# Cross-attention on one core: the output projection in three fp32r passes a block, and the splitting of queries and keys moved from VectorE to ScalarE

## What is computed

```python
q = heads(x @ to_q_w)                                   # (128, 128, 320) @ (320, 320)
for seg, (wk, wv) in zip(segments, weights):            # 77, 4, 4, 43 context rows, width 512
    out += merge(softmax(q @ heads(seg @ wk).T / 4) @ heads(seg @ wv))
result = out @ to_out_w + to_out_b + x                  # (320, 320)
```

## Time and profile before

| | |
|---|---|
| median of 3 runs | 1751.53 us (1750.83 to 1751.56) |
| profiled execution, its own time | 1750.32 us |
| span of its instructions | 1748.5 us |
| busy: PE, DVE, POOL, ACT | 1663.6, 1509.1, 1247.9, 1042.8 us |
| mean granted TensorE clock | 0.990 |

### The profile page before, as it was taken

One profiled execution on the slowest core, in us unless ns is written; L12 is line 12 of the kernel. 1 busy time (PEld: TensorE's weight loads), 2 busy tenths in 40 slices (PEclk: granted clock), 3 DMA queues, 4 the chain that ended last, 5 costly groups with the idle time before them and its releaser, 6 DMA issues.

```text
span 1748.5 us, 48271 instructions
## 1 busy us (share of the span) xinstructions
PE 1663.6 (95%) x15120; PEld 1370.2 (78%) x15120; DVE 1509.1 (86%) x3536; ACT 1042.8 (60%) x1860; POOL 1247.9 (71%) x1452
## 2 busy tenths in 40 slices
PE   6949999999999999999999999999999999999986
PEld 3647888888888888888888888888888888888865
DVE  4238999889999988999998899999889999988997
ACT  1126666666666666666666666666666666666664
POOL 4337777778777777877777887777788777778744
PEclk9979999999999999999999999999999999999999
DMA  8669888888988988898898889889889988987861
GB/s 294 173 168 222 205 221 220 216 219 217 227 201 221 222 215 216 220 224 204 220 224 213 213 222 222 205 222 226 211 213 225 218 208 220 227 209 195 214 128 39
DMA packets 409172, 366.24 MB, mean 209 GB/s; under 512 B 17137, under 2 KB 380210, under 8 KB 404786
## 3 DMA queue, kind: packets, MB, share of 16 engines
q1 hardware_dynamic: 409138, 365.79, 82.4%
HBM read 216.30 MB, written 149.42 MB: 209 GB/s over the span
## 4 chain that ended last, share of the span: by engine, by line
PE 88%; DVE 5%; issue 2%; DMA 1%; ACT 1%; SPq 1%; POOL 1%; ACTq 0%; POOLq 0%
PE job_ps L785 30%; PE ring_ps L851 15%; PE ring_ps L871 12%; PE ring_ps L864 10%; PE job_ps L801 7%; PE s_ps L824 7%; PE job_ps L804 2%; PE ring_ps L752 2%; PE job_ps L812 2%; DVE rest L657 1%; PE job_ps L795 1%; DVE l_seg L667 1%; ACT parts L523 1%; DVE probs L640 1%; DVE m_seg L624 1%
## 5 line engine op out<-in xcount | busy, mean ns | idle before, releaser
L463 POOL TENSOR_TENSOR probs<-probs,rl 128x616 f32<-128x616 f32 (+1 forms) x640 | 628.5, 1004 | 342.1 <-DVE rl L678 340.8
L785 PE MATMUL job_ps<-c_in,w_kv 128*128 128x172 f32 (+1 forms) x2560 | 576.7, 368 | 40.8 <-DVE rest L657 40.8
L550 ACT ACTIVATE pT<-ring_ps 128x512 f32<-128x512 f32 x640 | 378.2, 598 | 356.1 <-PE ring_ps L851 347.3
L785 PEld LDWEIGHTS job_ps<-c_in,w_kv 128*128 128x128 f32 x2560 | 424.4, 190 | 129.8 <-DVE rest L657 48.4
L851 PE MATMUL ring_ps<-ident,probs 128*128 128x128 f32 x2560 | 388.7, 277 | 9.7 <-DVE y L687 8.4
L667 DVE TENSOR_REDUCE l_seg<-probs 128x8 f32<-128x616 f32 (+1 forms) x640 | 385.2, 644 | 7.8 <-ACT probs L541 7.8
L640 DVE TENSOR_TENSOR probs<-s_ps,m_seg 128x616 f32<-128x616 f32 (+1 forms) x640 | 387.5, 647 | 0.0
L624 DVE TENSOR_REDUCE m_seg<-s_ps 128x8 f32<-128x616 f32 (+1 forms) x640 | 371.6, 623 | 3.5 <-issue 0.2
L541 ACT ACTIVATE probs<-probs 128x1024 f32<-128x1024 f32 x320 | 337.7, 1055 | 22.8 <-DVE probs L644 22.8
L851 PEld LDWEIGHTS ring_ps<-ident,probs 128*128 128x128 f32 x2560 | 290.0, 143 | 64.9 <-issue 25.6
L444 POOL TENSOR_TENSOR parts<-rest,zero 128x512 bf16<-128x512 f32 (+1 forms) x192 | 199.0, 1036 | 70.6 <-DVE rest L657 70.6
(11 more groups left out here) (47 smaller groups left out, 1457.0 us busy)
## 6 DMA issues: line engine op xcount, KB each, us to landing
q_all<-q_scratch SPq DMA_DIRECT2D x64, 960.0 KB, 8.4
k_all<-k_scratch SPq DMA_DIRECT2D x64, 960.0 KB, 12.4
c_in<-in_cT SPq DMA_DIRECT2D x32, 1024.0 KB, 5.1
x_raw<-in_xT SPq DMA_DIRECT2D x32, 768.0 KB, 5.1
q_scratch<-parts SPq DMA_DIRECT2D x64, 384.0 KB, 3.0
k_scratch<-parts SPq DMA_DIRECT2D x64, 384.0 KB, 3.0
x_res<-in_x SPq DMA_DIRECT2D x128, 160.0 KB, 3.4
out<-y SPq DMA_DIRECT2D x128, 160.0 KB, 2.8
```

Of the source, the lines that this page charges most:

```text
L463: pool.tensor_tensor(pr[:, :, a:e], pr[:, :, a:e], r[:, :, s:s + 1].broadcast_to((P, OH, e - a)), ALU.mult)
L550: act.activation(pT[:, h:h + QH, :], ring_ps[i][:, :].rearrange("p (h s) -> p h s", h=QH), ACT.Copy)\
L785: last = pe.matmul(dst[:, :, a:e], w_kv[:, l, k, i * P:(i + 1) * P], c_in[:, k, :, a:e], start=(k == 0), stop=(k == CK - 1))
```

## The change

The output projection is done in fp32r: `w_o` and each block's `oT` are cut into a rounded part and a remainder, and `project` does nine fp32r matmuls (three products for each of three pieces of the contraction) in place of three fp32 ones. ScalarE makes the rounded part (`oT_high`), GpSimd the remainder (`oT_low`). VectorE has no part in the splitting any more: ScalarE copies a query or key projection whole to SBUF, then writes part 1, later rounds the second part (`round_second`); GpSimd makes both remainders (`make_rest`, `make_third`). The bank is free after ScalarE's second copy.

```diff
@@ gpsimd
-            def split(g, n):
-                r = split_rows(n)
-                src, dst = rest[0:r, n % 2, :], parts[0:r, n % PR, :, :]
-                pool.wait_ge(part_freed, g * NSP + n + 1)
-                after(pool, parts_stored[n % PR], (g * (NSP // PR) + n // PR) * STORED)
-                pool.tensor_tensor(dst[:, 1, :], src, zero[0:r, :].broadcast_to((r, NB * S)), ALU.add)\
-                    .then_inc(part2_made, 1)
-                pool.wait_ge(part2_made, g * NSP + n + 1)
-                pool.tensor_tensor(dst[:, 2, :], src, dst[:, 1, :], ALU.subtract).then_inc(part3_made, 1)
+            def make_rest(g, n):
+                src = whole[0:r, n % 2, :]
+                pool.wait_ge(part1_made, g * NSP + n + 1)
+                pool.tensor_tensor(src, src, parts[0:r, n % PR, 0, :], ALU.subtract).then_inc(rest_made, 1)
+            def make_third(g, n):
+                pool.wait_ge(part2_made, g * NSP + n + 1)
+                pool.tensor_tensor(parts[0:r, n % PR, 2, :], whole[0:r, n % 2, :], parts[0:r, n % PR, 1, :],
+                                   ALU.subtract).then_inc(part3_made, 1)
...
+            for g in range(2):
+                for n in range(NSP):
...
+                    make_rest(g, n)
+                    make_third(g, n)
...
+            pool.wait_ge(wo_hi_made, 1)
+            pool.tensor_tensor(w_o[1][:, :, :], wo_raw[:, :, :], w_o[0][:, :, :].bitcast(fp32), ALU.subtract)\
+                .then_inc(wo_lo_made, 1)
+            def oT_low(b):
+                pool.wait_ge(oT_hi_made, b + 1)
+                pool.tensor_tensor(oT[1][:, :, :], oT_raw[:, :, :], oT[0][:, :, :].bitcast(fp32), ALU.subtract)\
+                    .then_inc(oT_lo_made, 1)
             def slot(g, n):
                 if live(g * NO + n - 1, G * NO):
                     scale(g if n else g - 1, (n - 1) % NO)
+                if n in VALUES_AT and live(g * NB + VALUES_AT[n], B):
+                    oT_low(g * NB + VALUES_AT[n])
                 for at in range(2):
-                    for turn, job in ended(g, n - 2, at):
+                    for turn, job in ended(g, n - 2 - at, at):
                         if job in SPLITS:
-                            split(turn + 2, SPLITS.index(job))
+                            make_third(turn + 2, SPLITS.index(job))
+                for at in range(2):
+                    for turn, job in ended(g, n - 1 - at, at):
+                        if job in SPLITS:
+                            make_rest(turn + 2, SPLITS.index(job))
@@ scalar, evacuate
+                    after(act, part3_made, g * NSP + m - 1)
+                    act.activation(whole[0:r, m % 2, :], ps[0:r, :], ACT.Copy)
                     after(act, parts_stored[m % PR], (g * (NSP // PR) + m // PR) * STORED)
                     act.activation(parts[0:r, m % PR, 0, :], ps[0:r, :], ACT.Copy).then_inc(part1_made, 1)
...
+            def round_second(g, m):
+                act.wait_ge(rest_made, g * NSP + m + 1)
+                act.activation(parts[0:r, m % PR, 1, :], whole[0:r, m % 2, :], ACT.Copy).then_inc(part2_made, 1)
...
+            def oT_high(b):
+                act.wait_ge(oT_copied, b + 1)
+                act.activation(oT[0][:, :, :], oT_raw[:, :, :], ACT.Copy).then_inc(oT_hi_made, 1)
...
+            waiting = None
             for turn, job in EARLY_JOBS:
                 evacuate(turn, job)
+                if job in SPLITS:
+                    if waiting is not None:
+                        round_second(*waiting)
+                    waiting = (turn + 2, SPLITS.index(job))
...
+            round_second(*waiting)
...
+            act.activation(w_o[0][:, :, :], wo_raw[:, :, :], ACT.Copy).then_inc(wo_hi_made, 1)
...
+                for at in range(2):
+                    for turn, job in ended(g, n - 2 - at, at):
+                        if job in SPLITS:
+                            round_second(turn + 2, SPLITS.index(job))
@@ vector
-            def subtract_part(turn, job):
...
-                dve.tensor_tensor(rest[0:r, m % 2, :], ps[0:r, :], parts[0:r, m % PR, 0, :], ALU.subtract)\
-                   .then_inc(part_freed, 1)
@@ tensor
-                        pe.wait_ge(part_freed, split_count(g, other))
+                        pe.wait_ge(part1_made, split_count(g, other))
...
             def project(b, i):
-                pe.wait_ge(oT_copied, b + 1)
+                pe.wait_ge(oT_lo_made, b + 1)
                 for k in range(3):
-                    last = pe.matmul(ring_ps[i][:, 0:C], oT[:, k, :], w_o[:, k, :], start=(k == 0), stop=(k == 2))
+                    for a, c in ((0, 0), (0, 1), (1, 0)):
+                        last = pe.matmul(ring_ps[i][:, 0:C], oT[a][:, k, :], w_o[c][:, k, :],
+                                         start=(k == 0 and (a, c) == (0, 0)), stop=(k == 2 and (a, c) == (1, 0)))
```

More of the change, by code:

```diff
@@ L169, in xattn_kernel @@
         w_q = [sb(f"w_q{i}", [P, 3, 3 * P], fp32r) for i in range(2)]
-        w_o = sb("w_o", [P, 3, C])
+        w_o = [sb(f"w_o{i}", [P, 3, C], fp32r) for i in range(2)]
         small = sb("small", [P, MKV, NB, NSM])
         ident = sb("ident", [P, P])
-        zero = sb("zero", [P, 1])
         parts = sb("parts", [P, PR, 3, NB * S], bf16)
-        rest = sb("rest", [P, 2, NB * S])
+        whole = sb("whole", [P, 2, NB * S])
         q_all = sb("q_all", [P, NPAIR * H * 2 * S], bf16)
@@ L186, in xattn_kernel @@
         rl = sb("rl", [P, 2, OH, NSEG])
-        oT = sb("oT", [P, 3, S])
-        y = sb("y", [P, 2, C])
+        oT_raw = sb("oT_raw", [P, 3, S])
+        oT = [sb(f"oT{i}", [P, 3, S], fp32r) for i in range(2)]
+        y_all = sb("y_all", [P, 3 * C])
+        y = y_all[:, 0:2 * C].rearrange("p (i c) -> p i c", i=2)
         pT_flat = pT[:, :, :].rearrange("p h s -> p (h s)")
@@ L241, in xattn_kernel @@
         oT_copied = sem("oT_copied")
+        oT_hi_made = sem("oT_hi_made")
+        oT_lo_made = sem("oT_lo_made")
+        wo_hi_made = sem("wo_hi_made")
+        wo_lo_made = sem("wo_lo_made")
         y_filled = sem("y_filled")
@@ L477, in _ @@
             pool.wait_ge(x_lo_made, CX)
[L478 to L485, removed]
+            for g in range(2):
+                for n in range(NSP):
+                    if (g, n) == (0, 3):
+                        for k in range(CX):
+                            x_low(1, k)
+                    make_rest(g, n)
+                    make_third(g, n)
             for k in range(CX):
                 x_low(2, k)
+            pool.wait_ge(wo_hi_made, 1)
[5 more added lines that the diff above has]
+                    .then_inc(oT_lo_made, 1)
             def slot(g, n):
@@ L600, in slot @@
                         copy_pT(g if what[0] >= 0 else g - 1, what[0] % NO, what[1], at % 2)
+                    if kind == "tr" and what[1] == 0 and n in VALUES_AT and live(g * NB + VALUES_AT[n], B):
+                        oT_high(g * NB + VALUES_AT[n])
                 for turn, job in ended(g, n, 0):
@@ L647, in shift @@
                    .then_inc(shifted, 1)
-            def subtract_part(turn, job):
-                g, m = turn + 2, SPLITS.index(job)
-                r = split_rows(m)
-                ps = job_ps[bank_of(turn, job)]
-                dve.wait_ge(part1_made, g * NSP + m + 1)
-                after(dve, part3_made, g * NSP + m - 1)
-                dve.tensor_tensor(rest[0:r, m % 2, :], ps[0:r, :], parts[0:r, m % PR, 0, :], ALU.subtract)\
-                   .then_inc(part_freed, 1)
             def sum_up(g, o):
@@ L684, in add_residual @@
                 dve.wait_ge(res_loaded[s % 2], (g * (NB // 2) + s // 2 + 1) * 16)
+                if isinstance(g, int) and g == 0 and s < 2:
+                    dve.wait_ge(wo_lo_made, 1)
                 after(dve, y_stored[s % 2], (g * (NB // 2) + s // 2) * 16)
@@ L712, in _ @@
                     reduce_max(0, 0)
-                if job in SPLITS:
-                    subtract_part(turn, job)
             dve.wait_ge(small_stored, 16)
@@ L727, in slot @@
                         add_residual(g + what // NB, what % NB, at % 2)
-                for at in range(2):
-                    for turn, job in ended(g, n - 1, at):
-                        if job in SPLITS:
-                            subtract_part(turn, job)
                 if live(gg, G):
```

28 lines of the change are left out of this document (16 added, 12 removed).

## The result

The changed kernel takes 1786.26 us (median of 4 runs, 1785.22 to 1786.83) where the kernel before took 1751.30 beside it: ratio 1.0199, 95% interval 1.0182 to 1.0217. The spans of the profiled executions are 1784.7 and 1748.5, 36.2 apart.

The account below looks back on a forecast made before the run. TensorE was taken as the bound (394.5 of 400 us busy). 1750.3 + 12 (groups) + 18 (before the loop) + 2.5 (first exponential) + 1 (end) = 1783.8, forecast 1785 us against the runs' median; range 1763 to 1815.

Parts of the forecast that it names:

- Output projection, 0.29 a block: Nine fp32r passes replace six records of 1.62 us and take 1.33: 0.29 saved a block, 1.16 a group.
- VectorE loses its 192 subtractions. That frees nothing on the path: VectorE's dropped subtractions save no time since TensorE is the bound; they only make shifts earlier.
- Slot 8, start of kv1, +0.7: ScalarE's whole copy of kv0 waits for GpSimd's third part behind `oT_low`; kv1 starts 0.7 us later, lower end -0.2.
- Slot 8 and slot 6 projections, +0.2 and +0.65: Output projections wait for ScalarE's delayed copy of the slot's first transposes: +0.2 us in slot 8, +0.65 in slot 6.
- the steady sum: A steady group: -1.16 + 0.7 + 0.2 + 0.65 = +0.39 us, times 30 groups +12 us.
- Before the loop, +18: Group 0's kv2 third part, 21.8 us later, holds SyncE's k store, pair load and small store: +18 us, bounds 9 and 21.
- First exponential, +2.5: ScalarE has 4.9 us more ahead of the first exponential, half covered by slack: +2.5 us, bounds 0 and 5.
- The end, +1: The last projection waits for the copy of `oT`, with `oT_high` and `oT_low` now between: +1 us.
- Rival 1: ScalarE's whole copies never wait for GpSimd, so both projection waits vanish and the kernel is faster: 1732 us; chance 0.10.
- Rival 2: Before the loop the small store overlaps and the wait is paid from TensorE's 19.3 us idle: 1767 us; chance 0.12.
- Rivals 3 and 4: In the projection, weight loads set the fp32r pace (1834 us, chance 0.08) or don't overlap the stream (some 1985, 0.02).
- Rival 5: Stacked pair loads, issued after later third parts, miss slot 8 by about 1 us a group: 1815 us; chance 0.06.

Follow-up runs that it names:

- e5: The changed kernel with its output projection put back to three plain fp32 matmuls, the splitting still moved to ScalarE; 1766.09 us.
- e9: The kernel before with only the output projection in fp32r, and GpSimd's split ahead of the output's remainder in its slot; 1723.11 us.
- e7: The changed kernel with both the early second part of kv2 of group 0 and GpSimd's third part ahead of `oT_low`; 1719.27 us.
- e2: The changed kernel with GpSimd making the third part ahead of `oT_low` in its slot, not behind it; 1734.33 us.
- e3: The changed kernel with three buffers for the whole copies instead of two, GpSimd's order unchanged; 1733.09 us.
- e1: The changed kernel with the second part of kv2 of group 0 rounded right behind its own read-out; 1771.27 us.
- e11: e7 with kv0 read out ahead of the copy of slot 7's second transposes, plus the rounding of `w_o` moved before the long stop; 1705.31 us.
- e8: e7 with part 1 made from the whole copy in SBUF, so the bank is free after one ScalarE copy; 1729.74 us.

## Why the prediction was right, step by step

The forecast, 1785, is 1.3 us off and the likeliest case held. That it is so close is luck, since its parts were off by more and cancelled: the groups cost 19.4 and not 12, the way to the first slot 8 16.0 and not 20.5, the end 0.85 (a remainder) and not 1. Both mechanisms, the wait in the group and the late store at the start, were the ones that the experiments show.

- *Output projection, 0.29 a block*: 0.30 measured. The pass takes 0.156, above both ends I gave (0.145 and 0.152), while the transposes ahead are followed 0.09 sooner. The fixed cost a pass, not one that goes with the columns, was the better reading, and it is 0.022. By the Trainium skill's gap (TensorE: Matmul & The Clock Gate, "Back-to-back issue gap") a block would take an estimated 1.22 us; 1.40 is measured.
- *"VectorE loses its 192 subtractions. That frees nothing on the path"*: nearly so as the kernel stood (e5: a group within 0.05), wrong as a rule. Once the projection is fast and the order mended, the new split is worth 0.12 a group on balance (e9 against e7).
- *Slot 8, start of kv1, +0.7*: 0.79. The predicted row held to the hundredth: from ScalarE's copy of the first transposes to the end of the third part 3.22 forecast, 3.21 measured. Order read off the program, with durations from the trace, was enough. That it is this wait is shown twice (e2, e3), and there kv1 starts 0.24 sooner than before the change, the lower end of -0.2.
- *Slot 8 and slot 6 projections, +0.2 and +0.65*: 0.25 and 0.84. With GpSimd's order mended the one in slot 6 falls from 1.28 to 0.61 and the one in slot 8 from 0.60 to 0.58 (e2). So the third part is 0.67 of slot 6's stop and next to nothing of slot 8's; 0.3 of what stays comes with the new split, since with the old one they are 0.52 and 0.36 (e9). kv1's 1.03 with these 0.67 and 0.02 make 1.72 of the 1.75 that a group gained.
- So the steady sum was mis-sized, +0.39 against +0.65, by three terms that were each too small; no term was missing. The saving was under-sized as well, 1.16 against 1.20, and took 0.04 of that back.
- *Before the loop, +18*: the mechanism is shown (e1 takes 15.0 off the time), the size was not right. The long stop ends 12.5 later, at 120.68 and not 126. The third part came out at 79.57, as worked out (79.25). But I put the small store's issue at 84.7 and its landing 19 later than before; the issue was at 89.5, since a `c_in` load ahead of it spent 4.96 us in issuing, and the landing only 15.3 later. It took 14.8 us from issue to landing, as before (14.1): adding the pair load's bytes to it was wrong. From that landing to the end of the stop are 16.4 us instead of 19.2. I had 0.7 of this, from the whole copy made in advance; e1 has 15.9 there. Which wait gives the other 2 us back wasn't tried. A 13.0 us wait of TensorE for `c_in` at 96.62 I did not foresee; it cost nothing of its own, since the long stop stands behind it.
- *First exponential, +2.5*: 3.45. Moving the rounding of `w_o` takes 0.9 off this wait and nothing off the time (e11). My sum was off here too: half of 4.9 - 1.3 is 1.8; 2.5 is half of the 4.9.
- *The end, +1*: 1.6. The last projection waits 1.63 longer, and from the values ahead of it (1741.63 before, 1776.24 after) to the end of the span are 6.9 and 8.5 us.
- *Range*: its lower end was added up wrongly. A group at -0.2 and a start of 10 give about 1757, not 1763; the measured time is far from it.
- The other marks: VectorE 331.9 (under 335) and GpSimd 332.5 hold; ScalarE was too high in my forecast (330; 302.9). PE's wait before kv1 was to be around 1.4 a group: its row has 1.47 (0.68 before), or 1.64 counted from the transposes' 0.44 on (0.85 before). The nine records are 0.156 apart, just outside 0.145 to 0.152.
- *Rival 1, third parts in time*: not what the changed kernel does, but what e2 makes of it. 1734.3 against 1732 worked out, which is luck again: the group gains 1.10 and not 1.36, since both projections still wait, and the way to the first slot 8 is 15.6 longer, not 20.5.
- *Rival 2, the start doesn't slide*: out; e1 alone brings the start back. *Rivals 3 and 4, weight loads set the pace or don't overlap*: out. Nine loads and nine passes take 1.40 us, with this in the groups of the changed kernel (busy, mean ns of one):

```profile
L907 PEld LDWEIGHTS ring_ps<-w_o,oT 128*128 128x128 f32 x1152 | 169.9, 188 | 44.7 <-ACT pT L579 42.1
```

The nine loads alone would be 1.69. The Trainium skill (same page, "The mechanism" in Part 3) lists that loads overlap running matmuls only when the row groups differ; the trace disagrees. The text above that list also lets a load go ahead that targets the background weight buffer; no run here shows whether that is what happens. *Rival 5, late stacked loads*: no wait for them between 200 and 1600 us in either trace.

## What to carry to other kernels

When work moves to another engine, read where it lands in that engine's program: an instruction whose input comes late, put ahead of one whose input has long been there, costs all that hangs on the second, though the engine has a sixth of its time free (GpSimd was busy 332.5 of 400 us). Test two edits apart as well as together: per group, one half of this change cost next to nothing (0.04 us) and the other gained 0.60, and the loss was made where they met. And before a loop, follow what the in-order DMA queue holds behind the store that comes late; here a part finished 22 us later cost 15 us.

## What the runs showed of the hardware

- An fp32r pass costs its columns at 2.4 GHz and about 0.02 us more: 0.156 us for 320 columns (0.133 and 0.022), 0.232 for 512 (0.213 and 0.018).
- A ScalarE copy from SBUF that waits for ScalarE's copy just ahead follows it by 0.63 us, where the two copies from a PSUM bank follow each other by 0.48 to 0.50 (e8 against e2 and after).
- GpSimd's subtraction into fp32r takes 1.005 us for 384 columns; 0.99 was worked out from 1.540 for 640 and 0.852 for 320.
- The issue of one DMA took SyncE 4.96 us in the changed kernel and 0.35 in e1 (at 75.01): issuing can itself be slow, and holds what is queued behind it. In the changed kernel it stands right behind the two issues of a pair load, in e1 6.6 us behind them. The kernel before has a slow issue in the same place, two `x_res` loads in 5.62 us (at 91.30). What it waited for the trace doesn't say.
